# Zero rows of the expert queue: written once from the counts of 8 token tiles, 9 blocks for each expert, in the last attention pass

## The reference

```python
def attention(x, context):                   # x is layernormed
    q, k, v = x @ Wq, context @ Wk, context @ Wv          # 16 heads of 64
    attn = softmax(q k^T * 64 ** -0.5)
    return (attn v) @ Wo + bo

def ffn(x):                                  # x is layernormed
    xf = (layernorm(x) * gamma + beta).reshape(-1, 256)   # 2048 tokens
    probs = clip(softmax(xf @ router_w.T), 1e-8, 1.0)
    topk_p, topk_i = top_k(probs, 2)
    for eid in range(8):
        xe = xf * dense_gate[:, eid:eid + 1]              # topk_p where chosen, else 0
        gate, up = split(xe @ gate_up_w[eid].T)
        out = out + (silu(gate) * up) @ down_w[eid].T
    return x + out

x = x + tanh(g_xattn) * attention(layernorm(x), ctx)
x = x + tanh(g_ffn) * ffn(layernorm(x))
```

## Time and profile before

| | |
|---|---|
| Median of 3 runs | 597.08 us |
| Lowest and highest | 595.59 and 599.96 us |
| Span of the profiled execution, first to last instruction | 602.2 us |
| Its own time without the profiler | not recorded |
| Mean granted clock of TensorE | 0.952 |
| PE busy | 522.3 us (87%) |
| DVE, ACT, POOL busy | 340.4, 282.2, 231.9 us |
| DMA, mean over the span | 69 GB/s, 41.54 MB |
| HBM written | 16.95 MB |

### The profile page before, as it was taken

One profiled execution on the slowest core, in us unless ns is written; L12 is line 12 of the kernel. 1 busy time (PEld: TensorE's weight loads), 2 busy tenths in 40 slices (PEclk: granted clock), 3 DMA queues, 4 the chain that ended last, 5 costly groups with the idle time before them and its releaser, 6 DMA issues.

```text
span 602.2 us, 12363 instructions
## 1 busy us (share of the span) xinstructions
PE 522.3 (87%) x3712; PEld 476.4 (79%) x3713; DVE 340.4 (57%) x783; ACT 282.2 (47%) x866; POOL 231.9 (39%) x319
## 2 busy tenths in 40 slices
PE   8999999999999999998998420699988998999991
PEld 6789999998989889898998410588877877888881
DVE  5856666677586585765756764255444544533330
ACT  3446556555465555564553112355543544533330
POOL 5160000337008780077704625043433433443333
PEclk9999999999999999999999755799999999999995
DMA  8500000001000100001010995636446436333322
GB/s 246 181 2 1 0 2 2 20 1 35 3 0 26 44 20 15 0 10 63 2 36 1 224 229 178 206 84 151 109 90 156 117 76 157 53 51 53 55 36 26
DMA packets 32372, 41.54 MB, mean 69 GB/s; under 512 B 3088, under 2 KB 28432, under 8 KB 32336
## 3 DMA queue, kind: packets, MB, share of 16 engines
q1 hardware_dynamic: 25184, 31.75, 17.9%
q0 software_dynamic: 7152, 9.33, 9.9%
HBM read 24.12 MB, written 16.95 MB: 68 GB/s over the span
## 4 chain that ended last, share of the span: by engine, by line
PE 34%; issue 26%; DVE 11%; ACT 8%; DMA 6%; POOL 6%; POOLq 3%; DVEq 2%; SPq 2%; another core or an unknown queue 1%; ACTq 0%
PE bank L603 7%; PE bank L581 6%; ACT probs L773 5%; PE bank L527 4%; POOL tok L1225 4%; PE bank L543 4%; PE bank L1279 3%; PE bank L557 3%; DMA expert_queue<-zrow 3%; DVE nmax L892 2%; POOLq L1233 2%; DMA out_dram<-yq,to_row 2%; PE bank L706 2%; PE bank L501 2%; DVEq L902 1%
## 5 line engine op out<-in xcount | busy, mean ns | idle before, releaser
L773 ACT ACTIVATE probs<-bank,nmax 128x154 f32<-128x154 f32 x256 | 97.6, 388 | 123.6 <-DVE nmax L892 119.3
L581 PE MATMUL bank<-vdiag,pT 128*128 128x128 f32 (+2 forms) x640 | 80.0, 272 | 7.1 <-DVE oT_lo L916 6.9
L581 PEld LDWEIGHTS bank<-vdiag,pT 128*128 128x128 f32 (+1 forms) x640 | 77.5, 191 | 10.5 <-DVE oT_lo L916 10.3
L1234 POOL DMA_INDIRECT out_dram<-yq,to_row x39 | 61.8, 1585 | 33.7 <-issue 24.1
L1279 PE MATMUL bank<-gu_hi,xqT_hi 128*128 x156 | 68.7, 441 | 1.1 <-DVE xqT_lo L1396 1.1
L892 DVE TENSOR_REDUCE nmax<-bank 128x2 f32<-128x308 f32 x128 | 60.1, 471 | 7.7 <-PE bank L543 6.8
L1279 PE MATMUL bank<-gu_hi,xqT_lo 128*128 x156 | 61.9, 397 | 0.0
L1279 PE MATMUL bank<-gu_lo,xqT_hi 128*128 x156 | 61.7, 396 | 0.0
L1408 DVE TENSOR_TENSOR hidT_lo<-bank,hidT_hi 128x512 fp32r<-128x512 f32 x39 | 26.9, 690 | 53.1 <-ACT hidT_hi L1355 53.1
L1403 DVE TENSOR_TENSOR hid<-hid,bank 128x512 f32<-128x512 f32 x39 | 26.8, 688 | 52.6 <-PE bank L1279 52.6
L557 PE MATMUL bank<-ident,probs 128*128 128x128 f32 (+1 forms) x320 | 46.2, 273 | 5.6 <-ACT xfT L786 2.9
(11 more groups left out here) (183 smaller groups left out, 1432.4 us busy)
## 6 DMA issues: line engine op xcount, KB each, us to landing
gu_raw<-in_gate_up_wT_dram SPq DMA_DIRECT2D x8, 1024.0 KB, 5.0
expert_queue<-zrow SPq DMA_DIRECT2D x8, 642.5 KB
xq<-expert_queue SPq DMA_DIRECT2D x39, 128.5 KB, 2.5
dn_raw<-in_down_wT_dram SPq DMA_DIRECT2D x8, 512.0 KB, 6.0
x<-in_x_dram SPq DMA_DIRECT2D x4, 512.0 KB, 13.0
out_dram<-out SPq DMA_DIRECT2D x8, 256.0 KB, 2.2
wq_raw<-in_L_xattn_Wq_dram SPq DMA_DIRECT2D x1, 1024.0 KB, 11.5
wo_raw<-in_L_xattn_Wo_dram SPq DMA_DIRECT2D x1, 1024.0 KB, 10.6
```

The lines of the kernel that those rows point to most:

```text
L581: last = nc.tensor.matmul(at[:, col0 + j0 * DH:col0 + j0 * DH + n], pT[u % 2][0:rows, b, :], v, start=(b == 0), stop=(b == NBLK - 1), skip ...
L773: last = nc.scalar.activation(probs[u % 4][:, j * NKB:(j + 1) * NKB], S_BANK[hf][:, m * NKB:(m + 1) * NKB], ACT.Exp, bias=nmax[:, u % 4, j ...
L1234: nc.gpsimd.indirect_dma_start(out[:, :], bass.IndirectOffsetOnAxis(to_row[:, 0:1], 0), yq[p % 2][:, :], None, compute_op=ALU.add).then_in ...
```

## The change

The starts are worked out from the counts of 8 tiles (blocks 1 and 2), which are known when the last pass begins, and `PAD_BLOCKS = 2 * TPI + 1 = 9` blocks are written for each expert: 8 for the rows that blocks 3 and 4 can bring, one to fill up. DVE's two steps move from behind the last pass to its head. SP issues the pads before the output of block 3. POOL's wait for `pads_q` moves from the rows of block 4 to those of block 3.

```diff
@@ -83,6 +83,8 @@
 
     RT = 2 * N // P // E
     LOOPS = MT // RT
+
+    PAD_BLOCKS = 2 * TPI + 1
     CHUNK = KF * D
     FIRST_CHUNKS = [(), (0,), (1, 2), ()]
 
@@ -297,15 +299,16 @@
                         dst = out[bass.ds((b * (SEQ // P) + 2 * i) * P, 2 * P), :].rearrange("(t p) d -> p t d", p=P)
                         sp.dma_start(dst, out0[:, 2 * b:2 * b + 2, :]).then_inc(s["out0_q"], 16)
 
-                with sp.Fori(0, NI - 1) as i:
+                with sp.Fori(0, NI - 2) as i:
                     send_output(i)
 
 
                 sp.wait_ge(s["pads"], 1)
                 for e in range(E):
-                    first = sp.value_load(pad[0:1, e:e + 1], min_val=0, max_val=DUMMY - (TPI + 1) * P)
-                    sp.dma_start(queue[bass.ds(first, (TPI + 1) * P), :].rearrange("(a p) d -> p a d", p=P),
-                                 zrow[:, :].unsqueeze(1).to_broadcast([P, TPI + 1, RW])).then_inc(s["pads_q"], 16)
+                    first = sp.value_load(pad[0:1, e:e + 1], min_val=0, max_val=DUMMY - PAD_BLOCKS * P)
+                    sp.dma_start(queue[bass.ds(first, PAD_BLOCKS * P), :].rearrange("(a p) d -> p a d", p=P),
+                                 zrow[:, :].unsqueeze(1).to_broadcast([P, PAD_BLOCKS, RW])).then_inc(s["pads_q"], 16)
+                send_output(NI - 2)
                 send_output(NI - 1)
                 sp.wait_ge(s["out0_q"], 32 * NI)
                 sp.wait_ge(s["zero_q"], 32)
@@ -469,6 +472,7 @@
                         send_rows(i, k)
                 body(NI - 1, more=False)
                 route_rstd(NI, 0, 0)
+                pool.wait_ge(s["pads_q"], 16 * E)
                 send_rows(NI - 1, 0)
                 route_rstd(NI, 1, 0)
                 for k in range(2):
@@ -478,7 +482,6 @@
                 number_tokens(NI)
                 nc.gpsimd.drain()
                 pool.wait_ge(s["gated"], 1)
-                pool.wait_ge(s["pads_q"], 16 * E)
                 for k in range(2):
                     send_rows(NI, k)
                 pool.wait_ge(s["rows_q"], 16 * 2 * NT)
@@ -1121,12 +1124,13 @@
                 with dve.Fori(1, NI - 1) as i:
                     for u in range(UPI):
                         slot(i, u)
+
+                dve.wait_ge(s["zero"], 1)
+                then(v.tensor_tensor(padf[:, :], base_cnt[:, :], region0[:, 0, :], ALU.add))
+                then(v.tensor_copy(pad[:, :], padf[:, :])).then_inc(s["pads"], 1)
                 for u in range(UPI):
                     slot(NI - 1, u)
 
-                dve.wait_ge(s["zero"], 1)
-                then(v.tensor_tensor(padf[:, :], base_cnt[:, :], region0[:, 0, :], ALU.add))
-                v.tensor_copy(pad[:, :], padf[:, :]).then_inc(s["pads"], 1)
                 scale_out(NI, -1)
                 block_stats(NI, 2)
                 for u in (0, 2):
```

## The result

| | before | changed |
|---|---|---|
| Median, 14 runs each | 599.35 us | 602.08 us |
| Lowest to highest | 595.59 to 601.46 us | 600.16 to 607.60 us |
| Ratio, 95% interval | | 1.0067 [1.0043, 1.0091] |
| Span of the profiled execution | 602.2 us | 605.8 us |
| Mean granted clock | 0.952 | 0.945 |

The ratio is not the quotient of the medians: these differ by 2.7 us, the means by 4.2 us. So by the ratios it costs 4 to 5 us where the prediction said -3.8; the time lies outside the range. The profiled execution of the changed kernel was the slowest of its 14 (607.6 us timed), so what its profile loses is more than the usual loss.

The account below looks back on a forecast made before the run. TensorE was taken to bound attention, and zero-row pad DMAs to delay the tail. The tail's -3.8 us, other terms 0, took the 602.2 us span to 598.4 and the 597.08 us median to 593.3; range 590 to 597.5.

Parts of the forecast that it names:

- Pads into the last pass: Last attention pass: the moved pad traffic lands with 16 and 24 us of cover before POOL's needs; 0 us.
- The tail's term, -3.8 us,: Tail before the expert stage: without pads, ACT's gating waits only for the choice and everything behind starts 3.8 us earlier.
- rival 1: Tail: something else replaces part of the wait, such as a row send slowed by weights; gain 2 us, 595.1 us; chance 0.08.
- DVE's two steps,: Pad address steps at the head of the last pass: bounds 0 and +0.4 us, taken as 0.
- the pads' landing: Last pass: all pads landed at 308 us, ahead of POOL's need of them at 332.57.
- rival 3: Last pass: pads land late and POOL waits at block 3's first send; 603.5 us at 130 GB/s; chance 0.03.
- the output behind them: SP's queue in the last pass: third block's output late by up to 8 us, nothing waits; 0 us.
- rival 2: Last attention pass: it pays for the traffic on its engines; +3.5 us, 596.8 us; chance 0.07.
- rival 4: Last pass: instruction code is fetched late under the pads; +16 - 3.8 us, 609 us; chance 0.03.

Follow-up runs that it names:

- e2: Changed kernel, pads early, with POOL's two drains in each block's first normalisation replaced by semaphore waits; ratio 1.0028 to the kernel before.
- e1: Changed kernel, but SP issues the pads only after the rows of blocks 1 and 2 have landed; ratio 0.9994 to the kernel before.
- f1: The kernel before, run and profiled once more unchanged; ratio 1.0005, span 596.8 us.
- g1: Changed kernel with pads held until block 2's rows landed and DVE's two pad steps moved into the last pass; ratio 0.9983 to the kernel before.
- f3: The kernel before with pads of 3 blocks in place of 5, still in the tail; ratio 0.9982.
- f2: The changed kernel, run and profiled once more unchanged; ratio 1.0090 to the kernel before.
- e3: The kernel before with POOL's two drains in each block's first normalisation replaced by semaphore waits; ratio 1.0025.
- e4: Changed kernel with 4 blocks a pad in place of 9; ratio 1.0024 to the kernel before.
- g2: The kernel before with POOL kept busy some 6.5 us ahead of block 3's first normalisation, no traffic added; ratio 1.0100.

## Why the prediction was wrong

**The step that failed** is "Pads into the last pass", which took 0 us for it. It asked who needs the rows of block 2 and found POOL's explicit wait at 324.24, 16 us of cover. It missed a second reader of that landing: the drain between `route_rstd` and the first `xin` step, at 279 us, which ends only when the rows that POOL sent are down (e2: none of the stall without the drain; e1: none with the rows landed first). The row for it was in reach: POOL idled 1.1 us there in passes 2 and 3, behind row sends, and 0.28 us in pass 1, before any, put down to "issue"; and the prediction itself said that row sends take 3.4 times as long beside the pads. Measured: a stall of 7.6 and 8.1 us in place of 1.1; 2.8 us of the 6.5 and 7.0 us more are covered by DVE's slack, 3.7 and 4.2 reach PE, and matmuls at half clock follow. Part B against f1: +7.0 and +4.3 us in the two profiles of the changed kernel. A fall of PE's clock in the last pass had no term in the prediction at all.

**The tail's term, -3.8 us,** had the right mechanism and a wrong size. Gating starts 0.2 us behind the choice, as said. But ACT's wait was 1.5 us longer than this in f1, not 3.8; the first profile had an early choice and late pads. And of what ACT gains a slower landing of the last row send takes some back, 4.2 and 5.0 us in place of 3.5, which has the outcome of rival 1. Its cause, the weights that start nearer to the sends, isn't shown: they were issued 8.0 us ahead of the last send in both profiles of the changed kernel, but also in g1, where the send landed in 3.6 us. Measured by part D of the table: -0.9 us and -0.1 us in the two profiles of the changed kernel, -1.4 us in f3 and -1.5 us in g1 at most. The median of the kernel before also lay 2 us higher in its full set of 14 runs than in the three shown, which alone would have moved the forecast.

**DVE's two steps,** bounds 0 and +0.4, taken at 0: 0.5 us at the first maxima, 0.3 us by the end of attention, inside the bounds (gone but for 0.2 us or less in g1). The idle 0.44 us two instructions on absorbed only part of them.

**Right:** the pads' landing, at 301.9 us where 308 was foreseen, was never waited for at 334 us, so rival 3 was not it; the output behind them made nobody wait; no engine ran slower for the traffic (e1: full queues and a full clock), so neither was rival 2; no stall in the last pass was one of code, so neither was rival 4, though it had the right sign and the right shape: a stall of one engine that a busy queue makes.

The sum by the runs, against f1: 7.0 (B: the stall and the clock behind it) + 0.5 (A: DVE's steps) - 0.9 (D: the tail) = 6.6 us in the first profile, 4.3 + 0.5 - 0.1 = 4.7 us in the second. Timed were 4.0 us (0.67%) and 5.4 us (0.90%). The sum leaves out part C, which was 1.6 us longer than in f1 in the first profile and 0.9 us shorter in the second; with it the sums are 8.2 and 3.8 us. Single profiles scatter by that much, and the sums show the direction and the rough size, no more. Part C, 33.4 to 36.1 us over all kernels, is 33.4 or 33.7 us where the first fall of PE's clock behind 310 us came at 333 us or later, and 34.2 us or longer where it came earlier. Whether the change has a share in that these runs can't tell.

**Open:** what made the two stalls of the first profile (A and B 5.5 us longer together than in f1) isn't known; they came in no other profile. In its timeline DVE's residual sum L923 idled 5.04 and 4.07 us there, put down to "remote", against 1.91 and 1.77 us for PE in f1. What the landing of the last row send goes by, 3.5 us in f1 and 5.0 in f2, is open too. Whether the remaining 0.2% of f3 and g1 is a gain the intervals don't tell.

## What to carry to other kernels

Before traffic is moved under idle queues, list everything that waits for a landing there, the implicit ones too: in these runs a drain on POOL behind the indirect DMAs that it had issued was a wait for their landing, and the profile put its idle time down to "issue". In front of such traffic, a semaphore wait on the DMAs already in flight is one line of code, and it took the stall away here (e1). And read a wait of a few us from more than one profile before selling it: here one execution showed 4.1 us where the next showed 1.7.

## What the runs showed of the hardware

- A drain on POOL behind indirect DMAs ended with their landing: 1.1 us of idle time in the kernel before, whose rows land in 2.7 us by e3, 4.6 us with 7.2 us (e4), 8.1 us with 8.9 us (f2); 0.1 us with semaphore waits in its place and rows still landing in 8.3 us (e2).
- PE's granted clock fell from 1.00 to 0.50 behind gaps of 3.7, 4.2 and 4.9 us, with full queues (changed kernel, f2) and with empty ones (g2), and stayed at 1.00 from 285 to 295 us at 282 and 301 GB/s without a gap (e1). Behind a gap of 0.7 us (e4) it didn't fall.
- Row sends of POOL beside a full SP queue of writes took 3 times as long to land as alone (8.3 to 8.9 us against 2.7). The Trainium skill (DMA: Bandwidth & Descriptors, Queues, rings and completion order) has each DMA engine take turns between queues by the packet. An estimate from that rule, with packets of like size in two queues, is twice as long; the measurement is above that.
